# One map layout for all passes of a Fourier layer tower, with two quads of maps handed from pass to pass on the chip

## The reference

```python
for i in range(L):                                   # L = 4
    x1 = _fourier_layer(v, W1, W2)                   # 12 + 12 x modes, 12 y modes are kept
    x2 = jnp.einsum('bcxy,cd->bdxy', v, w_w[i]) + w_b[i]
    v = x1 + x2
    mean = jnp.mean(v, axis=(0, 2, 3), keepdims=True)
    var = jnp.var(v, axis=(0, 2, 3), keepdims=True)
    v = (v - mean) * jax.lax.rsqrt(var + BN_EPS) * bn_g[i] + bn_b[i]
    if i < L - 1:
        v = jax.nn.relu(v)
```

## Time and profile before

| what | value |
|---|---|
| median of 3 runs | 1861.89 us (1854.05 to 1864.33) |
| the profiled execution | 1864.8 us, span 1862.9 us |
| TensorE matmul busy | 1422.1 us, 76% |
| weight loads (beside matmuls) | 816.5 us, 44% |
| VectorE | 687.8 us, 37% |
| ScalarE | 638.5 us, 34% |
| GpSimd | 287.6 us, 15% |
| moved by DMA | 346.46 MB in 168204 packets |
| mean granted TensorE clock | 0.813 |

### The profile page before, as it was taken

How to read it: one execution, slowest core, us unless ns; L and a number is a source line. 1 busy time by engine, 2 the same in 40 slices (tenths; PEclk the granted TensorE clock), 3 DMA queues, 4 the chain that set the end, 5 groups by cost and what they waited for, 6 DMA issues and landing times.

```text
span 1862.9 us, 46009 instructions
## 1 busy us (share of the span) xinstructions
PE 1422.1 (76%) x21279; PEld 816.5 (44%) x21279; DVE 687.8 (37%) x678; ACT 638.5 (34%) x918; POOL 287.6 (15%) x401
## 2 busy tenths in 40 slices
PE   3578599999848768787878478599998668816987
PEld 3334265666534334343434244255554354206841
DVE  6432245445412223332433322245553422057453
ACT  1232245555512224343444223155555422000140
POOL 4631301011031300101010231201011131000000
PEclk8778599999967668878888777589999979965576
DMA  3768556677547777878786368599999234930001
GB/s 96 157 175 260 170 175 190 181 189 196 201 120 217 220 233 217 242 217 236 223 227 199 96 188 251 169 316 316 316 297 319 92 92 148 392 81 1 1 0 23
DMA packets 168204, 346.46 MB, mean 186 GB/s; under 512 B 25748, under 2 KB 131604, under 8 KB 140100
## 3 DMA queue, kind: packets, MB, share of 16 engines
q1 hardware_dynamic: 152492, 306.46, 53.5%
q0 software_dynamic: 15520, 37.07, 8.0%
HBM read 173.58 MB, written 151.03 MB: 174 GB/s over the span
## 4 chain that ended last, share of the span: by engine, by line
PE 62%; ACT 11%; DVE 9%; DMA 7%; issue 6%; SPq 3%; POOL 1%; DVEq 0%; ACTq 0%
PE ps L1323 12%; PE ps L1285 6%; PE ps L1361 6%; PE ps L1262 6%; PE ps L1384 6%; PE ps L1357 4%; ACT ps L1163 4%; PE ps L1396 4%; PE ps L1344 4%; PE ps L1271 3%; ACT arena L1154 2%; DMA arena<-half_inverse 2%; PE ps L1442 2%; ACT arena L812 2%; PE ps L537 2%
## 5 line engine op out<-in xcount | busy, mean ns | idle before, releaser
L1154 ACT ACTIVATE arena<-ps,arena 128x1024 f32<-128x1024 f32 x192 | 221.7, 1202 | 420.0 <-PE ps L1361 251.0
L1674 DVE STREAM_TRANSPOSE arena<-ps 128x1024 f32<-128x1024 f32 x96 | 179.9, 1957 | 464.9 <-PE ps L1384 464.9
L1024 POOL DMA_DIRECT2D arena<-arena x192 | 110.7, 585 | 936.4 <-ACT arena L1171 934.1
L1660 DVE STREAM_TRANSPOSE arena<-arena 128x2048 f32<-128x2048 f32 x96 | 219.3, 2301 | 95.1 <-ACT arena L1154 57.9
L1163 ACT ACTIVATE ps<-ps 128x1024 f32<-128x1024 f32 x192 | 194.1, 1011 | 82.9 <-PE ps L1323 82.7
L1323 PE MATMUL ps<-arena 32*32 32x512 f32 x3072 | 194.6, 673 | 8.8 <-issue 8.8
L1262 PE MATMUL ps<-arena 64*64 64x64 f32 x2304 | 144.8, 285 | 63.3 <-DMA arena<-arena 63.3
L1285 PE MATMUL ps<-arena 48*128 48x512 f32 x288 | 128.9, 987 | 80.9 <-ACT arena L812 40.0
L1262 PEld LDWEIGHTS ps<-arena 64*64 64x64 f32 x2304 | 136.5, 166 | 122.3 <-issue 121.7
L1384 PE MATMUL ps<-arena 32*32 32x512 f32 x3072 | 169.7, 670 | 21.6 <-issue 19.7
L1361 PE MATMUL ps<-arena 48*128 48x128 f32 x2048 | 141.8, 291 | 22.9 <-DMA arena<-half_inverse 21.3
(11 more groups left out here) (275 smaller groups left out, 1225.9 us busy)
## 6 DMA issues: line engine op xcount, KB each, us to landing
maps<-arena SPq DMA_DIRECT2D x92, 1024.0 KB, 5.6
inputs<-maps SPq DMA_DIRECT2D x64, 1024.0 KB, 9.6
arena<-half_inverse SPq DMA_DIRECT2D x192, 192.0 KB
half_inverse<-arena SPq DMA_DIRECT2D x33, 1024.0 KB, 6.2
arena<-in_mode_w POOLq DMA_DIRECT2D x48, 384.0 KB, 3.7
arena<-maps SPq DMA_DIRECT2D x8, 2048.0 KB, 15.4
mixed_modes<-arena SPq DMA_DIRECT2D x72, 192.0 KB, 3.9
arena<-mixed_modes SPq DMA_DIRECT2D x36, 384.0 KB, 5.4
```

Source lines behind the costliest of these rows:

```text
L1154: nc.scalar.activation(half(h_out[q % 2], h)[:, 1024 * pair:1024 * pair + 1024], ps[:, 2 * pair:2 * pair + 2, :].rearrange("p b n -> p (b ...
L1660: nc.vector.transpose(dst, src).then_inc(h_turned, 1)
L1674: nc.vector.transpose(dst, src).then_inc(y_turned, 1)
```

## The change

Every pass now leaves its maps in one order, so each has the form with 128 output partitions, and the second table in `fx2` goes. The exchange of blocks moves into the loads. A load of half a map becomes four DMAs (`for j in range(QUAD)`), each with 128 rows of 512 floats, and its source is read with the column block g outside and the channel c inside.

Each pass begins with the two quads that the one ahead of it ended with. They stay on the chip: the slots of `h_in` and `h_out` change roles from pass to pass (`buf_a`, `buf_b`), and these two quads are neither stored nor loaded. The order of the quads is therefore another one in each pass (`UP`, `DOWN`, `BACK`), and pass l handles quad `ORDER[l][i]` at place i. The buffers for the modes in a mix (`bounce`) change sides too, and the waits for the map stores go from the mix to the pass.

```diff
+        UP = (*range(QUADS),)
+        DOWN = (14, 15, 12, 13, 8, 9, 10, 11, 4, 5, 6, 7, 0, 1, 2, 3)
+        BACK = (2, 3, 0, 1, *range(4, QUADS))
+        ORDER = (UP, DOWN, BACK)
+        KEPT = 2
+        MOVED = (QUADS - KEPT) // 2
+        def h_in(l, i):
+            return (buf_a, buf_b)[l % 2][i % 2]
+        def h_out(l, i):
+            return (buf_b, buf_a)[l % 2][i % 2]
...
-            def input_load(l, q, h):
-                sp.dma_start(half(h_in[q % 2], h), maps_d[l - 1, q, :, 2048 * h:2048 * h + 2048])\
-                  .then_inc(ld[q % 2][h], 16)
+            def input_load(l, i, h):
+                src = maps_d[l - 1, ORDER[l][i]].rearrange("p (h g n) -> h p g n", h=2, g=4)[h]
+                for j in range(QUAD):
+                    at = 2048 * h + 512 * j
+                    sp.dma_start(h_in(l, i)[:, at:at + 512],
+                                 src[32 * j:32 * j + 32].rearrange("c g n -> g c n")).then_inc(ld[i % 2][h], 16)
...
-                    if p == 0 and l:
-                        for q in range(2):
-                            sp.wait_ge(map_st[q], stores_before(l))
...
             def layer_pass(l):
-                for q in range(QUADS):
+                for s in range(2):
+                    sp.wait_ge(map_st[s], 32 * MOVED * l)
+                for i in range(QUADS - KEPT):
                     for h in range(2):
                         for pair in range(2):
-                            sp.wait_ge(a_free[pair], set_of(l, "out", q, h) + 1)
-                        if l < PASSES - 1 or q < QUADS - 2:
-                            sp.dma_start(maps_d[l, q, :, 2048 * h:2048 * h + 2048], half(h_out[q % 2], h))\
-                              .then_inc(map_st[q % 2], 16)
-                        if l and q + 2 < QUADS:
-                            input_load(l, q + 2, h)
-                        elif l + 1 < PASSES and q + 2 >= QUADS:
...
+                            sp.wait_ge(a_free[pair], set_of(l, "out", i, h) + 1)
+                        sp.dma_start(maps_d[l, ORDER[l][i], :, 2048 * h:2048 * h + 2048], half(h_out(l, i), h))\
+                          .then_inc(map_st[i % 2], 16)
+                        if l:
+                            input_load(l, i + 2, h)
+                    g_load(l, i + 2)
...
-                        if n == 0 and 0 < l < PASSES:
-                            for s in range(2):
-                                act.wait_ge(map_st[s], stores_before(l))
-                            act.wait_ge(h_turned, 2 * QUADS * l)
...
             def out_set(l, q, h):
                 s = q % 2
-                if l:
-                    pe.wait_ge(ld[s][h], 16 * (slot_use(l - 1, q) + 1))
-                if l:
+                if l and q >= KEPT:
+                    pe.wait_ge(ld[s][h], 64 * (MOVED * (l - 1) + q // 2))
                     for pair in range(2):
                         free_pair(l, "out", q, h, pair)
-                        blocks32(wbd[l], h_in[s], h, pair, False)
+                        blocks32(wbd[l], h_in(l, q), h, pair, False)
+                elif l:
+                    for pair in range(2):
+                        free_pair(l, "out", q, h, pair)
+                        for g in (2 * pair, 2 * pair + 1):
+                            at = 2048 * h + 512 * g
+                            nc.tensor.matmul(ps[:, g, :], wbd[l], h_in(l, q)[:, at:at + 512], start=True, stop=False)
...
-                            if layout(l):
-                                for x in range(4):
-                                    last = nc.tensor.matmul(ps[32 * x:32 * x + 32, b, at:at + 128],
-                                                            gtile[s][rows, 4 * x + 2 * h + n, 32 * b:32 * b + 32],
-                                                            iy[rows, :], start=False, stop=(i >= 2 and n == 1))
-                            else:
-                                last = nc.tensor.matmul(ps[:, b, at:at + 128], gtile[s][rows, 4 * b + 2 * h + n, :],
-                                                        iy[rows, :], start=False, stop=(i >= 2 and n == 1))
+                            last = nc.tensor.matmul(ps[:, b, at:at + 128], gtile[s][rows, 4 * b + 2 * h + n, :],
+                                                    iy[rows, :], start=False, stop=(i >= 2 and n == 1))
```

More of the change, by code:

```diff
@@ L52, in transform_tables @@
     fx[0, :, 1], fx[1, :, 1] = -np.sin(ang), np.cos(ang)
[L55 to L60, removed]
-                for s in range(2):
-                    fx2[layout, tile, i, s, :, s] = fx[:, x]
-    fx2 = fx2.reshape(2, 128, 192).transpose(1, 0, 2)
+    fx2 = np.zeros((SIDE, 2, 2, 2, 2, KX))
+    for s in range(2):
+        fx2[:, s, :, s] = fx.transpose(1, 0, 2, 3)
     order = (np.arange(4)[:, None] + 4 * np.arange(16)[None, :]).reshape(-1)
@@ L157, in tower_kernel, with bounce @@
         half = lambda tile, h: tile[:, 2048 * h:2048 * h + 2048]
-        h_in = [inputs[:, s * POSITIONS:(s + 1) * POSITIONS] for s in range(2)]
-        h_out = [view(A_OUT + s * POSITIONS, POSITIONS) for s in range(2)]
+        buf_a = [inputs[:, s * POSITIONS:(s + 1) * POSITIONS] for s in range(2)]
+        buf_b = [view(A_OUT + s * POSITIONS, POSITIONS) for s in range(2)]
+        def bounce(l):
+            return inputs if l % 2 else view(A_OUT, 2 * POSITIONS)
         modes = view(A_MODES, BATCH * 144).rearrange("p (b t y k) -> p b t y k", t=2, y=KYH, k=KX_HALF)
@@ L199, in tower_kernel @@
         fyt = take(64).rearrange("p (h n) -> p h n", h=2)
-        fx2 = take(384).rearrange("p (l r n) -> p l r n", l=2, r=2)
+        fx2 = take(192).rearrange("p (r n) -> p r n", r=2)
         ix = take(128)
@@ L853, in _, with head @@
             HEAD = 4 * QUAD * CHANNELS
+            def head(l):
+                at = ORDER[l][0] // 4 * HEAD
+                return at, at + HEAD
             def store_columns(ky, a, b, done):
@@ L907, in mix @@
                 sp.wait_ge(ix_head, 16 * (l + 1))
-                g_load(0)
-                store_columns(KY - 1, HEAD, 2048, ix_st[1])
+                g_load(l, 0)
+                store_columns(KY - 1, *((HEAD, 2048) if head(l)[0] == 0 else (0, 2048 - HEAD)), ix_st[1])
                 sp.wait_ge(ix_st[1], 16 * KYH * (l + 1))
-                g_load(1)
+                g_load(l, 1)
             def layer_pass(l):
-                for q in range(QUADS):
+                for s in range(2):
+                    sp.wait_ge(map_st[s], 32 * MOVED * l)
+                for i in range(QUADS - KEPT):
                     for h in range(2):
                         for pair in range(2):
-                            sp.wait_ge(a_free[pair], set_of(l, "out", q, h) + 1)
-                        if l < PASSES - 1 or q < QUADS - 2:
-                            sp.dma_start(maps_d[l, q, :, 2048 * h:2048 * h + 2048], half(h_out[q % 2], h))\
-                              .then_inc(map_st[q % 2], 16)
-                        if l and q + 2 < QUADS:
-                            input_load(l, q + 2, h)
-                        elif l + 1 < PASSES and q + 2 >= QUADS:
[L924 to L929, removed]
+                            sp.wait_ge(a_free[pair], set_of(l, "out", i, h) + 1)
[4 more added lines that the diff above has]
+                    g_load(l, i + 2)
             for l in range(PASSES):
@@ L942, in _ @@
             for s in range(2):
[L943 removed]
+                sp.wait_ge(map_st[s], 32 * MOVED * PASSES)
             for pair in range(2):
@@ L1278, in inverse @@
                 pe.wait_ge(kx_in[p % 2], 32 * (KYH // 2 * l + p // 2 + 1))
-                rows = kxin[p % 2].rearrange("k (o e b) -> k e o b", e=2, b=BATCH)
+                rows = kxin(l, p).rearrange("k (o e b) -> k e o b", e=2, b=BATCH)
                 for e in range(2):
@@ L1379, in y_transform @@
                         here = turned[rows, 2048 * yh:2048 * yh + 2048]
-                        if layout(l):
-                            src = here.rearrange("p (h j e x c) -> p h e x j c", h=2, j=4, e=2, c=32)[:, x // 2, x % 2]
-                        else:
-                            src = here.rearrange("p (h g n) -> p g h n", h=2, g=4)[:, x]
+                        src = here.rearrange("p (h g n) -> p g h n", h=2, g=4)[:, x]
                         last = nc.tensor.matmul(ps[32 * x:32 * x + 32, 4 + r, :], fyt[rows, yh, :], src,
```

53 lines of the change are left out of this document (24 added, 29 removed).

## The result

The changed kernel takes 2175.14 us (median of 4 runs, 2173.51 to 2179.56) against 1863.11 us (4 runs, 1854.05 to 1869.04): a ratio of 1.165, 95% interval 1.160 to 1.169. The forecast was 2195 us with a range of 2080 to 2320.

What follows compares the result with a forecast made beforehand. Pass 1 was taken as bound by TensorE, pass 2 by DMA engines and TensorE. Loads on four engines gave +117 us in pass 1 and +216 in pass 2, +333 on 1864.8, less 2.9: 2195 us, range 2080 to 2320.

Steps and rivals of the forecast that it cites:

- TensorE's gain in pass 1: L1357 goes from pass 1; if nothing else held it, pass 1 takes pass 2's 274.9 us, a gain of 98.8 us.
- Kept quads at 0: Two stores and two loads less at the pass ends, which the chain doesn't pass through: worth 0.
- The loads on four engines: New loads in passes 1 and 2 lie on 4 of 16 engines, 21.3 us per quad on each; chance 0.80.
- rival A: All 16 engines take the loads in passes 1 and 2: 1785 us, range 1755 to 1830; chance 0.16.
- My own hint from the rows: Issue table gives no landing time for 24, 3 or 8 rows outside, as if fewer engines took part.
- The sum: Each long pass: 5.8 us to first load, 14 x 32.8 us, 26 us to finish; 491 us, together +333 us.
- The price per quad: In passes 1 and 2 the four engines carry 11.5 us other traffic plus 21.3 us loads: 32.8 us.
- The upper bound: Dearer loads, or TensorE at 1.2 GHz taking some 34 us a quad: up to 37 per quad, 2313 us.
- Issuing: SyncE's load issues cost 0.43 us each; six more make 2.6 us per quad, hidden while the engines drain.
- Rivals B: Eight engines take the loads: 22.1 us per quad, each pass 341 us, 1895 us in all; chance 0.03.
- C: The change does nothing in all, pass 1's gain being eaten exactly, at 9.6 engines; chance 0.01.
- D: SyncE's 14 issues per quad become the bound, needing 1.2 us each; said to add nothing; no chance given.

Runs made afterwards that it cites:

- form 6: Changed kernel with one DMA of 128 rows x 2048 floats per half map, quads kept, exchange of blocks left out: 1784.57 us, ratio 0.954.
- form 7: Kernel before with one layout in all passes and nothing else, no quads kept, exchange left out: 1770.79 us, ratio 0.946.
- form 1: Changed kernel with the same exchange, each of the four DMAs filling 32 partitions, 32 outermost on both sides: 1832.66 us, ratio 0.981.
- form 2: Changed kernel with loads whose source has 8 x 16 rows, 8 outermost, channels permuted in place of the exchange: 1907.64 us, ratio 1.022.
- form 3: Changed kernel with four loads of 128 rows x 512 floats in the maps' own order, exchange left out: 1775.36 us, ratio 0.951.
- form 5: Changed kernel with two of the four loads of each half map left out, still 4 outermost: 1867.49 us, ratio 1.000.
- form 9: form 1 with its four DMAs issued for partition groups 0, 2, 1, 3: 1810.92 us, ratio 0.966.
- Form 10: form 1 with groups 0 and 1 loaded by SyncE's queue and 2 and 3 by GpSimd's: 1847.37 us, ratio 0.988.

## Why the prediction was right

1. *TensorE's gain in pass 1 (99 us).* Measured alone it is 102 us. In the change it is hidden, as the loads need 32 us per quad where TensorE needs 17. One row was overread on the way: 798 ns for 599 in L1323 was put down to the clock, but 0.84 for 0.99 makes 706 of 599. Nothing in the sum rests on it.

2. *Kept quads at 0.* Nothing on record contradicts the 0, as the intervals of forms 6 and 7 overlap. One detail was wrong: I wrote that their wide matmuls save under 2 us. They take longer than the narrow ones, 1.7 us more for a half at a clock of 1.00. Whether that is the whole of the 14 us between the medians of forms 6 and 7 is open: up to the second quad's second half (692.51 - 665.34 us and 691.98 - 667.15 us) form 6 is 2.3 us behind in pass 1, with the clock's rise at other places in the two.

3. *The loads on four engines.* This carried the forecast, and its doubt was the 0.16 for rival A. Forms 1 to 3 and form 5 answer it: with 4, 8, and 32 or 128 outside, with the same bytes, packets and number of loads, the time is 2175, 1908, and 1833 or 1775 us, the mean share follows the count, and half the bytes at 4 outside come near to all of them at 8. The rule of the Trainium skill (DMA: Bandwidth & Descriptors, "Why a DMA increments its semaphore by 16 and not by 1") fits here for unlike counts on the two sides: 4 on the DRAM side is enough, with 128 on the chip's side. No run has the small count on the chip's side alone. The traces count no engines by name; the four are inferred from the shares, the rates and the times.

   My own hint from the rows was weaker than I put it. The loads with 4 and with 8 outside have no landing time and those with 32 have one, but in the changed kernel the stores of 128 rows have lost theirs too. A blank there does not prove by itself that few engines took part.

4. *The sum.* 5.8 us before the first load and 26 us of tail were met (5.8 and 26.7). The price per quad was 32.8 and measured 32.0: 0.8 us in 28 quads makes 22 us, which is about the 20 us between forecast and result. The forecast of 150 GB/s was low; the stretch of pass 1 has 168.

   The clock was 0.74 in the stretch, and TensorE was busy 222.50 of 400 us, 17.8 us of the 32 of a quad, so it never became the slower of the two. The upper bound took a quad at 1.2 GHz as 34 us, from 144 of 318 matmuls in 17 us; these rows give 33 us by the 15.10 us that TensorE was busy and 38 by the whole stretch. It bore on the range alone.

   One term was too small and stayed hidden. Issuing was counted at 0.43 us a load, but the first four loads of form 3 (the upper line) take 3.21 us together, where form 6 has one:

```profile
673.34 3.21 SPq L906 DMA_DIRECT2D arena<-maps  x4
...
671.15 0.43 SPq L903 DMA_DIRECT2D arena<-maps  x1
```

   So the six more issues cost SyncE about 5.6 us per quad and not 2.6. With two stores and the half inverse, whose four loads take 1.72 us at the same place, its 14 issues take some 9 us of a quad's 17, and form 3 is not slower than form 6.

5. *Rival A's own price was too low.* It gave 1785 us, with 1755 to 1830. With 128 rows outside the time is 1775; with the exchange done, 1833, or 1811 in the better order. What I missed is that form 1, which gets 32 outside on both sides, fills only 32 partitions with each DMA, and that the engines then move 274 GB/s where they move 307 in form 3 at the same full share. The Trainium skill (SBUF — State Buffer, "Door 1: The DMA port swizzle") says that partitions 0 to 63 reach only half of the ports, so that groups 0 and 1 share a half and 0 and 2 don't. Form 9 agrees with a part for the halves (288 for 274 GB/s). Form 10 gives no support: with the halves fed from two queues it moves 268 GB/s and is slower than form 9. What holds the packets up was not settled.

Rivals B, C and D had no part. The times of the changed kernel and of form 2 lie on the two sums for four and for eight engines, the change did not come out at nothing, and form 3 with 14 issues a quad is not slower than form 6 with 8.

## What to carry to other kernels

Look at the order of dimensions of each side of a DMA before its bytes: by the prediction's estimate a small outermost count put 21 us of work on a quarter of the engines where 5 on all would do, and it looks in the profile like a held queue beside a half-idle DMA share. When a permutation moves from a compute engine into a load, price the load in its new shape, also for how many partitions each DMA fills. Time each half of a change alone: the single layout by itself was worth 5%, and the new loads by themselves cost 17%.

## What the runs showed that was not expected

- With loads that fill 32 partitions each, the engines move 274 GB/s at a DMA share of 1.02 in the middle of pass 1; with loads of 128 partitions it is 307 at 1.01, with the same 2 KB packets. For 16 partitions it is 257 at 1.03.
- The order of four such DMAs changes it: groups 0, 2, 1, 3 give 288 GB/s for 274, and the time is 22 us less. Spreading them over two queues gives 268.
- For a convolution with a block diagonal, 32 matmuls of 32 x 32 on different parts of the array take 2.02 us where 8 of 128 x 128 take 3.70 us, both with 512 columns. No kernel was timed with only this changed.
